# Zero-padded score operands, and the copy of the summed outputs on another engine, in the first attention layer of a four-layer kernel

## The reference

```python
for layer in range(4):
    x = x + layernorm(attn[layer](layernorm(x)))
    x = x + layernorm(ffn[layer](layernorm(x)))
```

```python
# attn[0]: bias[h] depends on (key - query) through a table of 32 buckets
q, k, v = split(z @ w_qkv.T)
p = softmax(q @ k.T * 8 ** -0.5 + bias[h])
out = merge_heads(p @ v) @ w_proj.T + b_proj
# attn[2]: learned tables of 63 clipped relative positions
s = q @ k.T * scale + q @ table_q[h][rel] + k @ table_k[h][rel]
p = softmax(s);  out = merge_heads(p @ v + p summed by rel @ table_v[h])
```

## Time and profile before

| | us |
|---|---|
| median of 3 runs | 2320.22 |
| range of the runs | 2318.97 to 2323.26 |
| the profiled execution | 2328.94 |
| its span | 2327.1 |
| PE busy, whole span | 1866.4 (80%) |
| DVE busy | 1692.1 (73%) |
| ACT busy | 1070.6 (46%) |
| GpSimd busy | 837.5 (36%) |
| first attention's loop at full clock, from 80.4 to 361.3 | 280.9 |
| third attention's loop, from 1424 to 1851 | 427.0 |

### The profile page before, as it was taken

The page is one execution under the profiler, slowest core; times in us unless marked ns, Lnnn a source line. Parts: engine busy times, 40 slices in busy tenths (PEclk is TensorE's granted clock), DMA queues, the critical chain, the costliest instruction groups (busy, mean ns, idle before and its releaser), DMA issues. The chain is left out here.

```text
span 2327.1 us, 46335 instructions
## 1 busy us (share of the span) xinstructions
PE 1866.4 (80%) x16408; PEld 1291.3 (55%) x16408; DVE 1692.1 (73%) x4008; ACT 1070.6 (46%) x2009; POOL 837.5 (36%) x637
## 2 busy tenths in 40 slices
PE   4999995688888885579999667887887759997756
PEld 2666663355555553367777534454554448886444
DVE  3899997676666676688999873988998772224574
ACT  1777773355554441134444333555555413332542
POOL 3000002875555511133444344444554217921111
PEclk8999997899999997779999965999998659998787
DMA  3111112000000000010000074444544350000000
GB/s 111 34 46 45 45 41 70 17 17 17 17 18 17 17 18 5 1 24 24 13 22 23 0 215 114 149 147 142 158 147 142 90 192 26 19 8 7 1 1 21
DMA packets 127630, 129.08 MB, mean 55 GB/s; under 512 B 75117, under 2 KB 103635, under 8 KB 126698
## 3 DMA queue, kind: packets, MB, share of 16 engines
q1 hardware_dynamic: 127466, 126.91, 18.4%
HBM read 78.59 MB, written 40.81 MB: 51 GB/s over the span
## 5 line engine op out<-in xcount | busy, mean ns | idle before, releaser
L2727 ACT ACTIVATE l2a_pr<-l2a_ps_s,l2a_nm 128x512 f32<-128x512 f32 x256 | 173.8, 685 | 130.1 <-DVE l2a_nm L2650 124.0
L454 ACT ACTIVATE l0a_pr<-l0a_sm,l0a_nm 128x512 f32<-128x512 f32 x256 | 185.1, 724 | 87.6 <-DVE l0a_nm L367 84.7
L367 DVE CUSTOM_DVE_ANT_0 l0a_sm<-l0a_ps_s,l0a_tb 128x512 f32<-128x512 f32 x256 | 176.1, 689 | 24.4 <-PE l0a_ps_s L522 9.1
L530 PE MATMUL l0a_ps_p<-top_c_ident,l0a_pr 128*128 128x128 f32 x1024 | 171.2, 291 | 0.0
L2650 DVE TENSOR_REDUCE l2a_nm<-l2a_ps_s 128x2 f32<-128x1024 f32 x128 | 156.7, 1224 | 4.4
L1612 POOL TENSOR_TENSOR l1f_h<-l1f_lm,l1f_sg 128x512 f32<-128x512 f32 x72 | 92.5, 1284 | 184.7 <-DVE l1f_lm L1676 184.7
L2657 DVE STREAM_TRANSPOSE l2a_tt<-l2a_pr 128x1024 f32<-128x1024 f32 x128 | 158.0, 1234 | 0.7 <-ACT l2a_pr L2727 0.6
L530 PEld LDWEIGHTS l0a_ps_p<-top_c_ident,l0a_pr 128*128 128x128 f32 x1024 | 109.7, 143 | 59.0 <-issue 45.8
L1738 ACT ACTIVATE l1f_csb<-l1f_ps_c,l1f_b3e 128x512 f32<-128x512 f32 x128 | 88.1, 688 | 108.2 <-PE l1f_ps_c L1524 107.9
L1991 ACT ACTIVATE l2f_h<-l2f_ps_h 128x512 f32<-128x512 f32 x128 | 76.4, 598 | 132.3 <-PE l2f_ps_h L1524 126.0
L1958 DVE SCALAR_TENSOR_TENSOR l2f_acc<-l2f_ps_y,l2f_comb,l2f_acc 128x128 f32<-128x128 f32 x112 | 31.6, 344 | 133.9 <-PE l2f_ps_y L2032 133.9
(11 more groups left out here) (531 smaller groups left out, 5120.4 us busy)
## 6 DMA issues: line engine op xcount, KB each, us to landing
l_qband<-l2a_staged SPq DMA_DIRECT2D x16, 768.0 KB, 15.7
l2a_qb<-l_qband SPq DMA_DIRECT2D x16, 768.0 KB
l2a_sb<-l_pband SPq DMA_DIRECT2D x32, 384.0 KB
l0a_tb<-l_bias SPq DMA_DIRECT2D x16, 448.0 KB
l2a_ks<-l_k SPq DMA_DIRECT2D x16, 384.0 KB
l_pband<-l2a_pr SPq DMA_DIRECT2D x32, 192.0 KB, 8.0
l_pband<-l2a_pr SPq DMA_DIRECT2D x32, 144.0 KB, 3.0
l2f_upw<-in_L_ffn_up_weights SPq DMA_DIRECT2D x9, 512.0 KB, 9.6
```

Of the source, the lines that this page charges most:

```text
L367: v.tensor_tensor_reduce(sm[j % 4][:, :], ps_s[j % 2][:, :], tb[slot][:, off:off + N][:, ::-1], -1.0, 3e38, ALU.add, ALU.min, nm[:, j % 4: ...
L454: a.activation(pr[j % 4][:, :], sm[j % 4][:, :], ACT.Exp, bias=nm[:, j % 4:j % 4 + 1], scale=-1.0).then_inc(m["p_ready"], 1)
L530: last = pe.transpose(ps_p[j % 4][:, tile(k)], pr[j % 4][:, tile(k)], ident[:, :])
L2727: a.activation(pr[slot][:, 2 * (g % 2) + u, :], ps_s[g % 2][:, u, :], ACT.Exp, bias=nm[:, g % 2, u:u + 1], accum_out=rs[:, n % 2, 2 * (g % ...
```

## The change

Three things change.

1. In `l0_attn`, the copy of the summed outputs (`ps_o` into `oc`) goes from DVE to ACT. It stays in step 2 of a group, where ACT issues it behind that step's exponential. The reciprocal (`invert`) and the multiplication no longer follow each other in one step: the reciprocal stays at lag 9, the multiplication goes to lag 10, with bias and maximum of the next step between them.
2. In `l0_attn`, `qs` and `ks` have 65 rows. GpSimd clears the four tiles before it starts on the parts, and SP waits for that before its first load. Rows 48 to 64 stay zero.
3. In `l2_attn`, `qs` and `ks` become two tiles of 65 rows, one for even and one for odd heads. Rows 51 to 64 are filled with zeros once, by four transfers ahead of the first head's loads.

The matmuls take as many columns as before; zero rows add nothing to the sums.

```diff
-L0_TR_LAG, ..., L0_OT_LAG, L0_NORM_LAG = 3, 4, 6, 7, 8, 9
+L0_TR_LAG, ..., L0_OT_LAG, L0_DEN_LAG, L0_NORM_LAG = 3, 4, 6, 7, 8, 9, 10
+FULL_ROWS = P // 2 + 1
-        qs = [s.sb(f"qs{i}", [KROWS, T * P], BF16) for i in range(2)]
+        qs = [s.sb(f"qs{i}", [FULL_ROWS, T * P], BF16) for i in range(2)]
         ... (ks alike)
+                sp.wait_ge(m["rows_zero"], 4)
                 ln.powers(g, B)
+                for rows in (*qs, *ks):
+                    g.memset(rows[:, :], 0.0).then_inc(m["rows_zero"], 1)
...
-                    v.tensor_copy(oc[b % 2][:, :], ps_o[b % 2]).then_inc(m["oc_ready"], 1)
+                def invert(g, b):
+                    o = ps_q[b % 2].rearrange("p (t w) -> p t w", w=VW)
+                    v.wait_ge(m["ot_ps"], g + 1)
+                    v.reciprocal(...).then_inc(m["rd_ready"], 1)
                 def normalize(g, b, h):
-                    v.wait_ge(m["ot_ps"], g + 1)
-                    v.reciprocal(r, o[:, :, HD:HD + 1]).then_inc(m["pool"], 1)
-                    v.wait_ge(m["pool"], g + 1)
+                    v.wait_ge(m["rd_ready"], g + 1)
...
+                def copy_out(g, b):          # on ScalarE
+                    a.wait_ge(m["pv_done"], g + 1)
+                    if not (isinstance(g, int) and g < 2):
+                        a.wait_ge(m["ot_ps"], g - 1)
+                    a.copy(oc[b % 2][:, :], ps_o[b % 2]).then_inc(m["oc_ready"], 1)
                     for j in range(2 * UNITS):
                         late(j, i, first)
                         exp(i * (2 * UNITS) + j, j)
+                        copy_step(j, i, first)
...
-        qs = s.sb("qs", [2 * (P // 2), T * P], BF16)
+        qs = [s.sb(f"qs{i}", [L2_ROWS, T * P], BF16) for i in range(2)]
+                    sp.dma_start(qs[i][FROWS:, :].rearrange(...), zero_rows ... broadcast_to([PAD, T, P]))
+                    sp.dma_start(ks[i][FROWS:, :, :].rearrange(...), zero_rows ... broadcast_to([PAD, 2 * T, P]))
-                            q = qs[r0:r0 + FROWS, b * N + GRP * a:b * N + GRP * (a + 1)]
+                            q = qs[h % 2][:, b * N + GRP * a:b * N + GRP * (a + 1)]
```

More of the change, by code:

```diff
@@ L256, in l0_attn @@
         va = s.sb("va", [P, T, HEADS, HD])
-        qs = [s.sb(f"qs{i}", [KROWS, T * P], BF16) for i in range(2)]
-        ks = [s.sb(f"ks{i}", [KROWS, T * P], BF16) for i in range(2)]
+        qs = [s.sb(f"qs{i}", [FULL_ROWS, T * P], BF16) for i in range(2)]
+        ks = [s.sb(f"ks{i}", [FULL_ROWS, T * P], BF16) for i in range(2)]
         tb = [s.sb(f"tb{i}", [P, W]) for i in range(2)]
@@ L375, in evac @@
                     v.tensor_copy(pT[j % RING][:, :], ps_p[j % 4][:, :]).then_inc(m["pTv"], 1)
[L377 to L381, removed]
-                    v.tensor_copy(oc[b % 2][:, :], ps_o[b % 2]).then_inc(m["oc_ready"], 1)
+                def invert(g, b):
+                    o = ps_q[b % 2].rearrange("p (t w) -> p t w", w=VW)
+                    v.wait_ge(m["ot_ps"], g + 1)
+                    v.reciprocal(rd[:, b % 2, :].unsqueeze(2), o[:, :, HD:HD + 1]).then_inc(m["rd_ready"], 1)
                 def normalize(g, b, h):
                     r, o = rd[:, b % 2, :].unsqueeze(2), ps_q[b % 2].rearrange("p (t w) -> p t w", w=VW)
-                    v.wait_ge(m["ot_ps"], g + 1)
-                    v.reciprocal(r, o[:, :, HD:HD + 1]).then_inc(m["pool"], 1)
-                    v.wait_ge(m["pool"], g + 1)
+                    v.wait_ge(m["rd_ready"], g + 1)
                     v.tensor_tensor(ao[:, b * NT:(b + 1) * NT, bass.ds(h * HD, HD)], o[:, :, 0:HD],
@@ L462, in evac, with copy_step @@
                     a.copy(pT[j % RING][:, :], ps_p[j % 4][:, :]).then_inc(m["pTa"], 1)
+                def copy_out(g, b):
[3 more added lines that the diff above has]
+                    a.copy(oc[b % 2][:, :], ps_o[b % 2]).then_inc(m["oc_ready"], 1)
+                def copy_step(j, i, first):
+                    g, e = divmod(j - L0_OC_LAG, NT)
+                    if e == NT - 1 and g < 2 * B and not (first and g < 0):
+                        copy_out(i * (2 * B) + g, g % B)
                 def late(j, i, first):
@@ L475, in _ @@
                     turn(i, False)
-                for j in range(2 * UNITS, 2 * UNITS + L0_EVAC_LAG):
-                    late(j, HEADS // 2 - 1, False)
+                for j in range(2 * UNITS, 2 * UNITS + L0_OC_LAG):
+                    if j < 2 * UNITS + L0_EVAC_LAG:
+                        late(j, HEADS // 2 - 1, False)
+                    copy_step(j, HEADS // 2 - 1, False)
                 for b in range(B):
@@ L2070 @@
 FROWS = KROWS + 3
+L2_ROWS = P // 2 + 1
+PAD = L2_ROWS - FROWS
 R_HALF = 31
@@ L2259, in _ @@
                 g.memset(zeros[:, :], 0.0).then_inc(m["zero_ready"], 1)
+                g.memset(zero_rows[:, :], 0.0).then_inc(m["pad_ready"], 1)
                 g.memset(rvd[:, :, :, :], 0.0).then_inc(m["zero_ready"], 1)
@@ L2438, in _ @@
                 pe.wait_ge(m["g_lo"], 1)
-        qs = s.sb("qs", [2 * (P // 2), T * P], BF16)
-        ks = s.sb("ks", [2 * (P // 2), 2, T * P], BF16)
+        qs = [s.sb(f"qs{i}", [L2_ROWS, T * P], BF16) for i in range(2)]
+        ks = [s.sb(f"ks{i}", [L2_ROWS, 2, T * P], BF16) for i in range(2)]
         rawk = [s.sb(f"rawk{i}", [P, T * P // HALF]) for i in range(2)]
@@ L2478, in head_scores @@
                         sp.wait_ge(m["s_ps"], PAIRS * (h - 1))
-                    first, sem = P // 2 * (h % 2), head_loaded[h % 2]
-                    sp.dma_start(qs[first:first + KROWS, :], q3[h * HD:(h + 1) * HD].rearrange("d c t -> (d c) t")).then_inc(sem, 16)
-                    sp.dma_start(ks[first:first + KROWS, :, :].rearrange("p v t -> p (v t)"),
+                    q, k, sem = qs[h % 2], ks[h % 2], head_loaded[h % 2]
+                    sp.dma_start(q[0:KROWS, :], q3[h * HD:(h + 1) * HD].rearrange("d c t -> (d c) t")).then_inc(sem, 16)
+                    sp.dma_start(k[0:KROWS, :, :].rearrange("p v t -> p (v t)"),
                                  k3[h * HD:(h + 1) * HD].rearrange("d c v t -> (d c) (v t)")).then_inc(sem, 16)
                     src = bass.AP(g3.tensor, g3.offset + h * 3 * T * P, [[T * P, 3], [HEADS * 3 * T * P, 2], [1, T * P]])
-                    sp.dma_start(ks[first + KROWS:first + FROWS, :, :], src).then_inc(sem, 16)
+                    sp.dma_start(k[KROWS:FROWS, :, :], src).then_inc(sem, 16)
                 def head_values(h):
```

23 lines of the change are left out of this document (13 added, 10 removed).

## The result

| | before | after |
|---|---|---|
| median of 5 runs of each, us | 2320.22 | 2337.97 |
| range of the runs | 2312.23 to 2323.26 | 2333.51 to 2339.72 |
| the profiled execution (its span) | 2328.94 (2327.1) | 2338.00 (2336.2) |

The ratio is 1.0078, with a 95% interval of 1.0056 to 1.0100: the change makes the kernel slower by 13 to 23 us, about 18. The profiled execution of before lies 5.7 us above the slowest of its timed runs, so the two profiles differ by only 9 us; what follows goes by stages. From the first to the last instruction that names a part's tiles, the first attention took 377.7 us before and 388.6 after, the second layer's feed-forward part 351.0 and 360.2, the third attention 548.8 and 542.3. The others differ by at most 3.4 us (the fourth attention, 130.3 and 127.0), and so much they scatter between profiles of kernels that leave them alone.

The account below looks back on a forecast made before the run. PE was taken to bound the first attention's loop, with nobody always busy in the third's. Terms +9.4 +2.3 -4 +1.5 gave +9.2 us: 2338.1 for the profiled execution, 2329.4 for the median; 8-in-10 range 2309 to 2347.

Parts of the forecast that it names:

- the clearing: Start of first attention: GpSimd's memsets slow two batches of DVE's normalization, +2.3 us (0 to 7.2, if they wait for all four).
- Rows: First attention's loop: 65-row scores share the transpositions' shape, saving shape changes; PE's work per group falls from 4.74 to 3.84.
- The first rival: First attention: 65 rows do not join the shape, nothing saved on PE, cycle 5.40, about 2363 us; chance 0.13.
- The cycle through ACT: First attention's loop: copy waits behind step 2's exponential, PE behind the copy; 4.90 us a group, 0.16 over before, +9.4 us.
- The second rival: First attention: the cycle through ACT is shorter than its parts; at 4.55 us a group, 2309 us; chance 0.15.
- the third: Terms cancel: first attention's cycle of 4.75 to 4.82 us with third attention's saving gives 2317 to 2324, no change; chance 0.17.
- The fourth: First attention's loop: PE's waits lower its clock to 0.9, 17 us more, 2346 us; chance 0.10.
- The early groups: First attention: the five groups before full clock, left at nothing; bounds -4.5 to +3.3 us.
- The third attention's loop: Third attention: 65-row scores shorten DVE's waits for PE, from 28.4 to 20 to 26 us; -4 us (0 to -10).
- The start: Third attention's start: four more transfers on SP's queue delay the first head's loads, +1.5 us (0 to +5).

## Why the prediction was right, and where it was off

The forecast was +9.2 us, 2329.4; measured are about +18 and 2337.97, inside the range. The mechanism of the first attention's loop is the one forecast; the clearing was mis-sized, the third attention's term is not confirmed, and two terms were missing: the place of DVE's code, and what the rows do to the clock at the start. That the working had 2338.1 for the profiled execution, which took 2338.00, is luck: in that one profile the third attention was 6.5 us shorter and the fourth, which was not touched, 3.4.

- *Rows.* Right: 0.22 instead of 0.31 after the scores. The first rival (65 rows don't join the shape) is out.
- *The cycle through ACT.* Right, and confirmed from both sides: 4.86 us, forecast 4.90 (the copy and its way to PE take 0.30, 204.75 to 205.05, and not 0.35); 5.35 without the rows, and 3.98 on average with the copy ahead of the exponential, where PE no longer waits for it. With what a turn adds at its branch, which the sum left out, the loss is 0.167 a group against the forecast's 0.16: two small errors that cancel. PE's busy share of the loop, 0.83, is near the 0.8 forecast. The second rival (a shorter cycle) and the third (all terms cancel) had the length of this cycle wrong; the third's 2317 also doesn't come out of its own terms, which give 2320.6 to 2324.7. The fourth's lower clock did not come: 1.00 over the loop.
- *The early groups*, left at nothing, gained: DVE's first branch back comes 78.2 us after the first scores before (54.81 to 133.06), 75.1 after (59.67 to 134.78), -3.1. That lies within the bound of -4.5, but not for its reason, PE's saving: the granted clock rose to 1.00 5.4 us after the first scores, and 14.7 before. An estimate of what this is worth, from two profiles with the first attention as before: 24.0 us at the low clock (the third attention alone, its first profile) against 14.7 make the same stretch 82.3 instead of 78.2, so 9.3 less are worth about 4.
- *The clearing.* The step that took one memset's wait for two batches, +2.3, failed: it cost 4.9. The four memsets follow each other without a gap, so DVE got through only when the last was over, 7.15 us for one batch: the case named as the upper end, in which DVE waits for all four; of the 6.0 us that the batch was longer, 1.2 did not reach the first scores. The rule of the Trainium skill cited there ("SBUF — State Buffer", Who interferes with whom) points this way: the loser waits for the other's whole instruction. The trace agrees in that DVE waited out whole memsets. Here it did not get in between two of them, though with the memsets first it did (12.48, above); why not here is not shown.
- *The third attention's loop*, -4: the step (shorter scores, shorter waits for them) was right and larger than forecast, 17.9 us of waits in the loop (54.8 less the first, 36.9) against 20 to 26; the gain is not confirmed by the timed runs (-2, -4.6 to +0.7, its later start included). The start, +1.5, was right (+1.2).
- *Missing: the place of DVE's code*, +9.2. No term stood for it, since the sum took parts that the diff doesn't touch as unchanged.

Put together: +4.9 for the start, -3.1 for the early groups, +8.0 for six turns of the loop (6 x 1.34) and about +0.9 at its end, +9.2 for the code, -2 for the third attention are +17.9, beside a measured 18. All but the last are from one profile of each kernel, whose untouched parts differ by up to 3.4 us, so that the sum meets the 18 so closely is in part chance.

## What to carry to other kernels

Moving work to an engine with time to spare helps only if nothing ahead of it in that engine's order waits for something later than the work itself needs: here two neighbouring lines on ScalarE decide between 18 us lost and 44 gained. Sum every cycle of waits that passes through the moved instruction, not only each engine's busy time. And compare the profiles part by part, the untouched parts too: a shorter program on one engine can move a later loop to a place where it is slower.

## What the runs showed of the hardware

- A DVE loop of 268 instructions stood 3.1 us longer at its branch back, each time, when 36 instructions ahead of it were gone, or 92 more were put in; with the 36 put back it did not. 36 less and 92 more are 128 apart. Why it depends on the place was not measured. PE, idle for 3.06 us by it, then had a granted clock of 0.54 for 3.4 us.
- Four GpSimd memsets in a row held four short DVE instructions for 7.15 us instead of 1.11; in another kernel a DVE instruction of 4 columns was held by one memset of the four only (0.84 us instead of 0.17).
- ACT's copy of 128 columns let the next instruction start 0.14 us later (204.75 to 204.89), though it is listed with 0.25; before the exponential it took 0.27.
- The granted clock of TensorE rose from 0.50 to 1.00 (1.2 to 2.4 GHz) 5.4 to 8.6 us after the first scores of the first attention where their operands had 65 rows (eight profiles), 14.7 to 24.0 us after them where they had 48 (six). Why was not measured.
